# Edge convolution of a four-layer graph network: message pieces read in place, one-hot rows moved to ScalarE

## What is computed

```python
message = relu(node_feats[edge_index[1]] + edge_feats)          # [100000, 64]
message_reduce = segment_sum(message, edge_index[0], num_nodes)
h = (1.0 + eps) * node_feats + message_reduce
```

## Time and profile before

| | us |
|---|---|
| median of 3 runs | 3908.64 |
| the runs | 3887.22 to 3921.21 |
| profiled execution | 3911.47 |
| its span, first to last instruction | 3909.7 |

### The profile page before, as it was taken

The page is one execution under the profiler, slowest core; times in us unless marked ns, Lnnn a source line. Parts: engine busy times, 40 slices in busy tenths (PEclk is TensorE's granted clock), DMA queues, the critical chain, the costliest instruction groups (busy, mean ns, idle before and its releaser), DMA issues. The chain is left out here.

```text
span 3909.7 us, 58497 instructions
## 1 busy us (share of the span) xinstructions
PE 1851.2 (47%) x16222; PEld 1337.5 (34%) x16222; DVE 2229.1 (57%) x4872; ACT 1212.0 (31%) x3818; POOL 1585.0 (41%) x1665
## 2 busy tenths in 40 slices
PE   6745555555545555411322247841111565655287
PEld 5633333333333333310111146741100455544222
DVE  7777777777777777311201023341100799997899
ACT  1155454544444544300011012100000233335644
POOL 1055555555555555466766630046667100000000
PEclk9865565555565565655655569875555788896599
DMA  7711222222122212622222200044443122221000
GB/s 248 304 42 43 45 43 43 46 42 43 43 43 45 42 42 48 246 63 51 61 53 54 52 23 1 12 114 109 128 113 73 60 77 78 78 81 35 0 0 9
DMA packets 399308, 267.12 MB, mean 68 GB/s; under 512 B 321456, under 2 KB 349293, under 8 KB 399073
## 3 DMA queue, kind: packets, MB, share of 16 engines
q1 hardware_dynamic: 306278, 87.81, 10.6%
q10 hardware_dynamic: 41472, 118.96, 8.4%
q0 software_dynamic: 51488, 59.40, 6.0%
HBM read 158.59 MB, written 107.47 MB: 68 GB/s over the span
## 5 line engine op out<-in xcount | busy, mean ns | idle before, releaser
L1237 POOL DMA_INDIRECT sorted_edges<-r_load,r_to x800 | 787.8, 985 | 674.3 <-DMA r_to<-places 375.3
L807 POOL DMA_INDIRECT hsrc<-h,edges x808 | 775.3, 960 | 596.0 <-PE ps L1004 363.7
L1004 PE MATMUL ps<-AO,hsrc 125*64 125x64 f32 x1616 | 195.9, 316 | 300.7 <-remote 245.0
L1049 PE MATMUL ps<-hot,lo 125*128 125x400 bf16 (+2 forms) x1000 | 273.6, 456 | 101.9 <-DVE hot L866 67.5
L1415 PE MATMUL ps<-R,w_work 128*128 128x64 bf16 x3000 | 155.3, 207 | 333.1 <-issue 186.7
L875 DVE TENSOR_TENSOR prod<-ps,hsrc 125x1024 f32<-125x1024 f32 x200 | 244.3, 1221 | 114.9 <-issue 107.9
L1031 PE MATMUL ps<-rwin,there 120*125 120x256 bf16 x800 | 182.7, 404 | 246.9 <-DVE there L850 230.0
L1004 PEld LDWEIGHTS ps<-AO,hsrc 125*64 125x64 f32 x1616 | 179.9, 224 | 336.9 <-issue 336.9
L1552 ACT ACTIVATE R<-w_work 128x384 bf16<-128x384 f32 (+1 forms) x160 | 85.8, 536 | 654.4 <-DVE w_work L1754 576.2
L1754 DVE TENSOR_TENSOR w_work<-ps,w_work 128x384 f32<-128x384 f32 (+1 forms) x160 | 91.2, 570 | 345.3 <-remote 342.5
L866 DVE TENSOR_SCALAR hot<-ramp,small 125x400 bf16<-125x400 int16 x800 | 211.6, 322 | 132.0 <-issue 128.0
(11 more groups left out here) (411 smaller groups left out, 3919.4 us busy)
## 6 DMA issues: line engine op xcount, KB each, us to landing
w_work<-sorted_edges ACTq DMA_DIRECT2D x42, 1000.0 KB
r_load<-in_edge_attr_dram SPq DMA_DIRECT2D x80, 312.5 KB
dstrow<-dst_rows SPq DMA_DIRECT2D x101, 234.4 KB
sorted_edges<-A ACTq DMA_DIRECT2D x10, 2000.0 KB, 9.8
A<-counts SPq DMA_DIRECT2D x12, 1600.0 KB
counts<-A ACTq DMA_DIRECT2D x4, 4000.0 KB, 31.8
sorted_edges<-A ACTq DMA_DIRECT2D x15, 1000.0 KB, 9.6
hsrc<-h,edges POOLq DMA_INDIRECT x808
```

What stands on the lines that cost most here:

```text
L807: g.indirect_dma_start(out=hsrc[:, s, t, :], out_offset=None, in_=S.h0[:, :], in_offset=bass.IndirectOffsetOnAxis(ap=edges.bitcast(I32)[:, ...
L1004: mm = pe.matmul(sums.rearrange("d (h w) -> d h w", h=H)[:, :, OFF[t]:OFF[t] + SUB], hsrc[0:TP, s, t, :], AO[0:TP, t, :, :], start=(t == 0 ...
L1049: mm = pe.matmul(S.ps[:, at0 + c0:at0 + c1], lo[0:TP, s, t, :], hot[0:TP, t, c0 - k0:c1 - k0], start=(t == FIRST[k]), stop=False, skip_gro ...
L1237: g.indirect_dma_start(out=S.sorted, out_offset=bass.IndirectOffsetOnAxis(ap=to[:, hf, t:t + 1], axis=0), in_=load[:, hf, t, :], in_offset ...
```

## The change

The high and middle pieces are no longer written. A float32's upper 16 bits are a bf16, so the scatter reads the upper halves of `msg` (now rectified in place by ScalarE) and of `left` (the remainder) with a step of two 16-bit values; only the lowest piece is written, packed. ScalarE's cast falls away, and VectorE's remainder becomes a plain subtraction. `there` stays on VectorE for group 3 alone. For groups 0, 1 and 2 ScalarE makes the rows, two groups ahead, as relu(1 - (value - partition)^2), by a Square and a Relu. TensorE's broadcasts run three groups ahead and are issued behind the scatter. The loop for the remaining edges gets pieces of its own (`omp`).

```diff
+    BYACT = GN - 1
...
-    mp = S.R[:, 1116:1116 + GB * SP3 * D].bitcast(BF16).rearrange("p (s b d f) -> p s b d f", s=2, b=GB, d=SP3)
+    left = S.R[:, 1116:1116 + 2 * GB * D].rearrange("p (s b f) -> p s b f", s=2, b=GB)
+    low = S.R[:, 1116 + 2 * GB * D:1116 + 3 * GB * D].bitcast(BF16).rearrange("p (s b f) -> p s b f", s=2, b=GB)
+    upper = lambda t: t.bitcast(BF16).rearrange("p s b (f u) -> p s b f u", u=2)[:, :, :, :, 1]
+    mp = (upper(msg), upper(left), low)
+    omp = view(6340, 6340 + SP3 * D // 2).bitcast(BF16).rearrange("p (d f) -> p d f", d=SP3)
...
+    row_of = view(6676, 6677)
...
@@ TensorE
             pe.wait_ge(qm["oht"], 1)
+            for b in range(size(2)):
+                c = GROUPS[2][0] + b
+                mm = pe.transpose(spans[0][:, b * P:(b + 1) * P], dl[:, 0, c:c + 1].to_broadcast([P, P]), S.identb[:, :])
+            mm.then_inc(qm["bc"], 1)
...
-                        pe.wait_ge(qm["oht"], i * GN + n + 1)
+                        if n % GN < BYACT:
+                            pe.wait_ge(qm["oht"], i * BYACT + n // GN * BYACT + n % GN + 1)
+                        else:
+                            pe.wait_ge(qm["ohv"], i + n // GN + 1)
...
-                                mm = pe.matmul(acc[:, GROUPS[n][0] + b, :], lo[:, k, b, :], mp[:, k, b, d, :], start=False, stop=False,
+                                mm = pe.matmul(acc[:, GROUPS[n][0] + b, :], lo[:, k, b, :], mp[d][:, k, b, :], start=False, stop=False,
...
                     for n in range(GN):
                         gather(n + 1)
-                        broadcast(n + 2)
                         scatter(n)
+                        broadcast(n + 3)
...
@@ ScalarE
+            def hot_rows(g, bc, made):
+
+                k, w = g % 2, size(g) * P
+                act.wait_ge(qm["bc"], bc)
+                nc.scalar.activation(ohT[:, k, 0:w], spans[k][:, 0:w], ACT.Square, bias=pidx[:, 0:1]).then_inc(qm["square"], 1)
+                act.wait_ge(qm["square"], made)
+                nc.scalar.activation(ohT[:, k, 0:w], ohT[:, k, 0:w], ACT.Relu, bias=pidx[:, 1:2], scale=-1.0).then_inc(qm["oht"], 1)
+
+            hot_rows(0, 1, 1)
+            hot_rows(1, 2, 2)
...
-                        act.wait_ge(qm["sc"], i * GN + g + 1)
                         act.wait_ge(qm["x"], i * GN + g + 1)
-                        nc.scalar.activation(mp[:, k, 0:m, 0, :], msg[:, k, 0:m, :], ACT.Relu).then_inc(qm["hi"], 1)
-                        act.wait_ge(qm["rem"], i * GN + g + 1)
-                        act.copy(mp[:, k, 0:m, 1, :], msg[:, k, 0:m, :]).then_inc(qm["mid"], 1)
+                        nc.scalar.activation(msg[:, k, 0:m, :], msg[:, k, 0:m, :], ACT.Relu).then_inc(qm["hi"], 1)
+                        if (g + 2) % GN < BYACT:
+                            hot_rows((g + 2) % GN, i * GN + g + 3, i * BYACT + (g + 2) // GN * BYACT + (g + 2) % GN + 1)
                         if g == 1:
                             chunk = chunk_of(i + 2)
...
@@ VectorE
-            own.step(v.tensor_copy(pidx[:, 0:1], pidxI))
+            own.did(v.tensor_scalar(pidx[:, 0:1], pidxI, -1.0, None, ALU.mult))
+            own.did(v.memset(pidx[:, 1:2], 1.0))
+            own.step(v.tensor_copy(row_of, pidxI))
...
                 w = size(n) * P
-                v.tensor_scalar(ohT[:, k, 0:w], spans[k][:, 0:w], pidx[:, 0:1], None, ALU.is_equal).then_inc(qm["oht"], 1)
+                v.tensor_scalar(ohT[:, k, 0:w], spans[k][:, 0:w], row_of, None, ALU.is_equal).then_inc(qm["ohv"], 1)
...
-            there(0, 0, 0)
...
                         v.wait_ge(qm["hg"], i * GN + n + 1)
+                        v.wait_ge(qm["sc"], i * GN + n + 1)
                         v.tensor_tensor(msg[:, k, 0:m, :], S.bank[2 + k][:, 0:m * D].rearrange("p (b f) -> p b f", f=D),
                                         es[:, s, cols, 0:D], ALU.add).then_inc(qm["x"], 1)
-                        there(1 - k, n + 1, i * GN)
+                        if n + 2 == BYACT:
+                            there(k, n + 2, i * GN)
                         v.wait_ge(qm["hi"], i * GN + n + 1)
-                        v.scalar_tensor_tensor(msg[:, k, 0:m, :], msg[:, k, 0:m, :], 0.0, mp[:, k, 0:m, 0, :], ALU.max, ALU.subtract
-                                               ).then_inc(qm["rem"], 1)
-                        v.wait_ge(qm["sc"], i * GN + n + 1)
+                        v.tensor_tensor(left[:, k, 0:m, :], msg[:, k, 0:m, :], mp[0][:, k, 0:m, :], ALU.subtract).then_inc(qm["rem"], 1)
                         v.tensor_tensor(lo[:, k, 0:m, :], ramp1b.unsqueeze(1).to_broadcast([P, m, P]),
                                         over(slo[:, s, cols], [P, m, P]), ALU.is_equal).then_inc(qm["lo"], 1)
-                        v.wait_ge(qm["mid"], i * GN + n + 1)
-                        v.tensor_tensor(mp[:, k, 0:m, 2, :], msg[:, k, 0:m, :], mp[:, k, 0:m, 1, :], ALU.subtract).then_inc(qm["low"], 1)
+                        v.wait_ge(qm["rem"], i * GN + n + 1)
+                        v.tensor_tensor(low[:, k, 0:m, :], left[:, k, 0:m, :], mp[1][:, k, 0:m, :], ALU.subtract).then_inc(qm["low"], 1)
...
```

More of the change, by code:

```diff
@@ L1141, in spread @@
     props = [{n: sem(f"c_{n}{k}") for n in ("prod", "free", "own", "sum") if (n, k) != ("sum", 1)} for k in range(4)]
-    cl = {n: sem("k_" + n) for n in ("tp", "xt", "y", "t", "y1", "yfree", "hi", "r", "mid", "lo", "out", "wd", "carrier")}
-    qr = {n: sem("r_" + n) for n in ("sc0", "sc1", "ready", "carrier", "acarrier")}
+    cl = {n: sem("k_" + n) for n in ("tp", "xt", "y", "t", "y1", "yfree", "hi", "r", "mid", "lo", "out", "wd")}
+    qr = {n: sem("r_" + n) for n in ("sc0", "sc1", "ready", "carrier")}
     qm = {n: sem("m_" + n) for n in (
-        "es0", "es1", "hw0", "hw1", "spot0", "spot1", "const", "consti", "own", "own2", "dl", "bc", "oht", "hg", "x", "hi", "rem", "mid", "low", "lo",
+        "es0", "es1", "hw0", "hw1", "spot0", "spot1", "const", "consti", "own", "own2", "dl", "bc", "oht", "ohv", "square", "hg", "x", "hi", "rem", "low", "lo",
         "sc", "seeded", "oes", "oidx", "ohg", "ob", "ob_free", "omsg", "o_free")}
@@ L1322, in turn_block @@
                 pe.wait_ge(cl["xt"], b + NB)
-                pe.sem_inc(cl["carrier"], 1)
+                pe.sem_inc(qr["carrier"], 1)
                 pe.transpose(S.bank[5][0:D, 0:P], fresh[:, m, :], S.ident[:, :]).then_inc(cl["tp"], 1)
@@ L1428, in _ @@
                         for d in range(SP3):
-                            mm = pe.matmul(acc[:, GROUPS[n][0] + b, :], lo[:, n % 2, b, :], mp[:, 0, 0, d, :], start=False, stop=False,
+                            mm = pe.matmul(acc[:, GROUPS[n][0] + b, :], lo[:, n % 2, b, :], omp[:, d, :], start=False, stop=False,
                                            skip_group_check=True)
@@ L1563, in _ @@
                 act.wait_ge(qm[f"es{s}"], n * 16 + 16)
-            act.sem_inc(qr["acarrier"], 1)
+            act.sem_inc(qr["carrier"], 1)
         @block.vector
@@ L1794, in _ @@
                 mine.step(v.tensor_scalar(omsg, omsg, 0.0, None, ALU.max))
[L1795 to L1798, removed]
+                mine.step(v.tensor_copy(omp[:, 0, :], omsg))
+                mine.step(v.tensor_tensor(omsg, omsg, omp[:, 0, :], ALU.subtract))
+                mine.step(v.tensor_copy(omp[:, 1, :], omsg))
+                mine.step(v.tensor_tensor(omp[:, 2, :], omsg, omp[:, 1, :], ALU.subtract))
                 v.sem_inc(qm["omsg"], 1)
```

## The result

The changed kernel takes 3961.1 us (median of 4 runs, 3948.9 to 3965.4); the kernel before takes 3904.0 (4 runs). The ratio is 1.0137, 95% interval 1.0113 to 1.0161: slower by 57 us, where 57 were forecast. The sum came out right with some terms that did not; what follows takes them apart.

The account below looks back on a forecast made before the run. In the second stretch VectorE's remainder waits on ScalarE's Relu round trip, which bounds each group. +1.32 us an item at full clock and +0.26 for the lower clock, together +1.58 x 36 = +57 us, gave 3966 us; range 3915 to 4008.

Parts of the forecast that it names:

- The three one-hot operations cost nothing to remove: VectorE, three groups an item: 1.6 us of one-hot work inside ScalarE's Relu round trip, its going costed at nothing.
- Group 1 waits for the broadcast, +0.72 at the full clock: VectorE's `there(3)` waits for TensorE's broadcast behind the scatter: start at 1.40 us, remainder at 1.92 instead of 1.20.
- The register load delays group 3, +0.35: ScalarE, group 2 into 3: next Relu 2.29 us after the second Relu's start, waiting 1.41 us where it waited 1.06.
- Rival A: ScalarE is serial: register loads or DMA issues start only after the last activation ends; +90 us, 3999 us; chance 0.20.
- The DMA issues delay group 0, +0.25: ScalarE, group 3 into 0: three DMA issues before the next Relu, which waits 1.00 us where 0.75 is usual.
- The cast's removal costs nothing: ScalarE's middle-piece cast and VectorE's wait for it go: nothing, since the lower rows' 0.87 us covered it.
- The lower clock adds 1.0 us in 26% of the time: TensorE at 1.2 GHz: slower scatter and transposes before `there` and Squares, +1.0 us an item, 26% of time, +0.26.
- The first stretch stays, within 12 us: From 2612 to 3045 us, beside GpSimd's scatters, 16 of 160 groups pass: left at 433 us, 12 us either way.
- the full clock's sum: Second stretch, per item: group 1 +0.72, group 3 +0.35, group 0 +0.25, together +1.32 us at the full clock.
- Rival B: Small loss: register load and DMA issues fit their gaps, only `there(3)` costs; 3922 to 3935 us; chance 0.20.
- Rival C: VectorE's queue is the bound after all, the remainder starting right behind the sum; -56 us, 3853 us; chance 0.05.
- Rival D: Pieces read in place slow TensorE's scatter, 0.36 us before each broadcast; +14 on the forecast, 3981 us; chance 0.10.

Follow-up runs that it names:

- e10: The changed kernel run again, unedited, on a chip of the first kind: 3968.8 us, 1.0156 of before.
- e1: Changed kernel with TensorE's broadcast put ahead of the scatter again, still three groups ahead: 3917.5 us, 1.0034 of before.
- all three edits: Changed kernel with broadcast ahead of scatter, both register loads behind group 1, VectorE's lower one-hot rows ahead of its Relu wait: 3847.2 us, 0.9834; other chip kind 0.9972.

## Why the prediction was right

The forecast was +57 us from +1.58 us an item; measured are +57 us between the medians and +1.45 an item (36 items, 52 us, which is also the difference of the two profiled executions). The mechanism was right: VectorE's work went and bought nothing, and the item grew by waits for a broadcast, a register load and the lower clock. By its steps:

- *The three one-hot operations cost nothing to remove.* Right: group 2 went from 3.02 to 2.96 us. Filling the idle time (2.40) shows that it was the round trip and no other engine.
- *Group 1 waits for the broadcast, +0.72 at the full clock.* Right: `there` starts 1.39 us behind the sum, and group 1 takes 4.65 us in the second item of a turn, where it took 3.95: +0.70. Swapping two lines removed it. The working was looser than its result: its three terms add up to 1.34, not 1.40, and the earlier trace rows have the scatter 0.23 behind the sum, not 0.21. In a turn's first item group 1 takes 4.82; the other 0.17 us stand behind `begin`'s small operations, and were not foreseen.
- *The register load delays group 3, +0.35.* Right in its place and near in price: the load takes 2.28 us from the activation's start, and group 3 went from 3.41 at its shortest to 3.66, +0.25. Rival A, ScalarE serial, is excluded by that 2.28: by the earlier trace rows the next Relu would come 0.53 us later, as the activation (1.04) is longer than the cast (0.51). Rival A's own sum took "0.9 later" for each of two chains but added it once; 0.9 is about what the two give together (0.53 and 0.43).
- *The DMA issues delay group 0, +0.25.* Right in half of the items only. The 2.00 us came from a row ahead of a turn's first item and held the end of the loop's turn as well; there the way now takes 1.94 us, and group 0 goes from 3.47 to 3.60, +0.13. Inside a turn it takes at most 1.67 us, the Relu is on time, and group 0 goes from 3.40 to 3.34. The mean is +0.03. Whether the loop's end itself makes the difference, no run isolates; the items of a turn differ in their buffers too.
- *The cast's removal costs nothing.* Too small a claim: it is a gain. The first half of the change, alone, is worth 0.71 us an item, since the register load also moves forward with it and each Relu starts 0.06 us sooner.
- *The lower clock adds 1.0 us in 26% of the time.* The size was near: where the lower level falls on group 1, that group takes 5.44 us for 4.65, or 5.61 for 4.82, +0.79, and in e10 items that it hits take about 16.15 for 15.02 and 15.6 for 14.6. The share was wrong. It was taken from the trace of before (0.87 granted), but with the change the granted clock was 0.75, half of the time at the lower level. This term was 15.29 - 14.82 = 0.47 us, not 0.26.
- *The first stretch stays, within 12 us.* Right: 1 us.

So the full clock's sum was +1.00 us (14.82, the mean of 14.62 and 15.02, against 13.82), not +1.32, and the clock's +0.47, not +0.26. Two errors of 0.3 and 0.2 us nearly cancel, and the medians lie 5 us further apart than the traces. That the forecast met the loss to the microsecond is luck; that it lay near is not.

Rival B (only `there` counts) falls with e1: there `there` waits no more, yet group 3 still takes 3.67 us and the kernel is 0.34%, 13 us, above before. Rival C falls with group 2. Rival D, the strided read, falls too: the pieces alone are faster than before, and 21 scatter matmuls of that kernel, at the full clock, run from 3202.10 to 3202.88, 0.78 us against the 0.77 of the earlier trace rows:

```profile
3202.10 0.19 PE L1421 MATMUL ps<-w_work 128*128 128x64 bf16 x1 [1.34 <-DVE R L1776]
...
3202.66 0.22 PE L1421 MATMUL ps<-R,w_work 128*128 128x64 bf16 x2
```

The Trainium skill (SBUF — State Buffer, Door 1: The DMA port swizzle) says that accesses inside one 16-byte line run at full bandwidth, by which a step of 4 bytes is free; this 0.78 agrees. The Trainium skill's rule to use VectorE for relu and simple arithmetic (ScalarE: Activation LUTs, Rules for kernel authors) holds here for the time of one operation, 0.61 against 0.88 + 0.94 us, and not for this kernel's: with the waits out of the way, the slower engine's rows bring 0.8 us an item.

## What to carry over

Before an operation is moved off the busiest engine, look at what that engine waits for just behind it: if the operation lies inside another engine's round trip, its removal is worth nothing until something else is put there. Count on the receiving engine what sits in its queue between two answers that others wait for, register loads and DMA issues included, which no busy time shows. Read such a cost from every place in the loop's turn, not from one row. And two lines' order on a third engine, free before, can carry most of the loss once its product is needed one step sooner.

## What was not expected

The granted clock moved with the waits. With nearly the same TensorE instructions an item, it was 0.87 before, 0.75 changed (0.78 in the second run), 0.69 with the loads moved, 0.82 with the order mended, 0.91 with the pieces alone and 0.88 with the rows ahead; what in the pattern of its waits decides this, the runs don't settle. What the lower level costs depends on where it falls, not on its share of the item: in the changed kernel items at 0.67 took 15.1 us and items at 0.77 took 15.6, the latter with the lower level at group 1's broadcast. Where the broadcast stood ahead of the scatter (e1) it cost next to nothing: group 1 took 3.88 us at a granted clock of 1.00 and at 0.74, and items alternated between 13.8 and 14.2 us, the two items of a turn. The kernel before took 13.8 to 14.1 us at 0.62 to 0.65, and 13.8 at 1.00.

Chips differ more than kernels: before took 3901 and 3911 us on two and 2882 and 2881 on two others. In the first stretch on the first kind 730 matmuls pass in 433 us, with TensorE waiting on instruction issue, and 859 in the kernel with all three edits; on the second kind this last one passes 5266 in 440 us beside the same scatters:

```profile
1860.00:2300.00 440.00, 255.32 (x5266) 239.80 (x5263) 339.97 (x633) 222.92 (x300) 342.81 (x299) 0.77 0.57 157
```

Why issue is so slow on one chip and not on the other no run here shows.
